# First cross attention: the last group of batches is projected in two tiles of four batches, the first tile's products placed ahead of the last two batches' probabilities

## The chip, the cores and the metric

The kernel runs on one core of a Trainium2 chip. The metric is the device time of one execution in microseconds; the figure that counts is the median of several executions.

## The reference: what is computed

Two layers over x (64 batches of 32 rows, 256 wide) with a context of 257 rows per batch. Each layer is a cross attention, a self attention and a feed-forward part, each added to x. The change lies in the first cross attention alone. Its latents are the layer-normed rows of x, its keys and values come from the normed context and from the latents themselves, with 16 heads of 64:

```python
xn = layernorm(x, ln_x_g, ln_x_b)            # context, 257 rows
ln = layernorm(latents, ln_l_g, ln_l_b)      # 32 rows
q = (ln @ Wq).reshape(b, m, h, d).transpose(0, 2, 1, 3)
kv = jnp.concatenate([xn @ Wkv, ln @ Wkv], axis=1)
kv = kv.reshape(b, n + m, 2, h, d)
k = kv[:, :, 0].transpose(0, 2, 1, 3)
v = kv[:, :, 1].transpose(0, 2, 1, 3)
qn = rmsnorm(q, qn_g) * scale
kn = rmsnorm(k, kn_g)
sim = jnp.einsum('bhid,bhjd->bhij', qn, kn)
...
attn = jax.nn.softmax(sim.astype(jnp.float32), axis=-1).astype(sim.dtype)
out = jnp.einsum('bhij,bhjd->bhid', attn, v)
out = out.transpose(0, 2, 1, 3).reshape(b, m, h * d)
return out @ Wout + bout
```

## The kernel before

The program is a row of stages; each has one stream of instructions per engine, written out by hand with semaphores, and ends in a barrier of all engines. The stage of the change is `cross_keyed`. The next is `self_attention`, whose first work on every engine stands behind that barrier.

`cross_keyed` goes through 64 batches (`n`) in 8 groups (`g`) of 8 (`GB`, place `j`). The values are never formed: the probabilities are multiplied with the normed context rows (`mix`), which gives 256 numbers per head and query, and the value and output weights are applied to a whole group at once (`project`). The order of the work on an engine is the order in which `group` calls the helpers. While batch n is finished, the batches behind it are prepared: keys of batch n+2 (`f.keys`, L382), transposed context rows of n+3 (L364), the spread of the key norms of n+1 (L409 transposes, L418 spreads them over the score columns through the two banks `key_bank`, ACT copies them out at L345), and raw rows of n+4. In the last group nothing of a next group is prepared (`is_in` is false past its end), so batch 62 has no keys to compute beside it, and batch 63 neither keys nor norms.

For one batch the chain is: `scores(n)` on PE (L1297, L1302) at the end of the batch before; maxima on DVE (L1112, L1115); exponentials on ACT (L1235); reciprocal and scaling on DVE (L1119, L1124) and the tail of the probabilities on POOL (L1200, L1202); transposes of the probabilities on PE (`probs_T`, L1313); high parts by ACT (L1242, L1244) and low parts by DVE (L1129, L1133); two times seven products on PE (`mix`, L1328), one half of the features each; both halves copied to the tile `mix` by ACT (L1249). POOL computes the key norms two batches ahead (L295, a power, then a split in three parts, L174 to L181).

After the eighth batch `project` (L1331 on) applies the value weights: four steps `i`, each with two pairs of heads, in the banks `key_bank[0]` and `key_bank[1]` in turn,

```python
mm = nc.tensor.matmul(key_bank[i % 2][half * DH:(half + 1) * DH, (pr % 2) * GT:(pr % 2 + 1) * GT],
                      wm.wv[:, f, h * DH:(h + 1) * DH], m.mix[:, f, place(h), :], start=(f == 0), stop=(f == FC - 1),
```

32 products of 256 tokens, with ACT copying the even steps to `oT` (L1278) and DVE the odd ones (L1164). Then the output weights: 2 tiles of 128 tokens, 8 products each (L1353), in the banks `out_bank` (banks 4 and 5 of the eight). Bank 4 is also the second bank of `mix`, bank 5 the one in which key norms are summed and transposed (`norm_bank`). DVE adds each tile to the residual (L1173). In all groups but the last the norm statistics for the next stage follow (`after.tile`); those of the last group are taken inside the next stage.

## Time and profile before

| | us |
|---|---|
| median of 3 runs | 2615.75 (2612.44 to 2619.3) |
| span of the profiled execution, first to last instruction | 2599.8 |
| time of the profiled execution | none is shown beside its span |
| PE busy | 2439.1 (94%) |
| DVE, POOL, ACT busy | 1696.2 (65%), 1474.8 (57%), 1282.3 (49%) |
| mean granted TensorE clock | 0.976 of full |

What stands in brackets behind a row is how long the engine was idle before it, and what ended that. The span does not hold the whole of a measured time: start and end of the program lie around it.

### The profile page before, as it was taken

How to read it: one execution, taken by the hardware profiler on the slowest of the kernel's cores; microseconds unless marked ns; L12 is line 12 of the kernel's file. 1: busy time of each engine (PE TensorE's matmuls, PEld its weight loads, DVE VectorE, ACT ScalarE, POOL GpSimd, SP SyncE). 2: the span in 40 equal slices, each digit the busy share in tenths (PEclk: the TensorE clock that was granted, in tenths of full speed). 3: DMA queues.
4: the chain of work that ended last, by engine and by line, in shares of the span. 5: the costliest groups of instructions: out<-in, count | busy, mean ns of one | idle time of the engine just before them, and what ended most of it. 6: DMA issues, size and time to landing. Idle time of an engine off the chain costs nothing. (4 is left out here: it accounts for less than half of the span.)

```text
span 2599.8 us, 64316 instructions
## 1 busy us (share of the span) xinstructions
PE 2439.1 (94%) x24498; PEld 1902.3 (73%) x24513; DVE 1696.2 (65%) x3969; ACT 1282.3 (49%) x2972; POOL 1474.8 (57%) x1669
## 2 busy tenths in 40 slices
PE   6998999999999999998797999699999999998997
PEld 3456888878787878886565588578888888886665
DVE  5777878686867777774575844476656655653665
ACT  3665656565656565654342333254445444543343
POOL 6996757676767576764662254675456544332233
PEclk9999999999999999998997999799999999999998
DMA  5332211111112121110003469533234323210001
GB/s 186 122 139 61 61 40 40 40 44 37 48 32 50 32 48 36 44 32 8 30 5 106 132 194 309 176 112 87 71 83 102 86 68 85 72 45 15 3 4 35
DMA packets 224819, 190.03 MB, mean 73 GB/s; under 512 B 89218, under 2 KB 212675, under 8 KB 224515
## 3 DMA queue, kind: packets, MB, share of 16 engines
q1 hardware_dynamic: 208994, 153.92, 19.9%
q0 software_dynamic: 9216, 27.28, 4.4%
q10 hardware_dynamic: 6304, 4.72, 0.6%
q8 instruction: 198, 3.24, 0.5%
q14 instruction: 107, 0.87, 0.1%
HBM read 151.53 MB, written 34.31 MB: 71 GB/s over the span
## 5 line engine op out<-in xcount | busy, mean ns | idle before, releaser
L295 POOL TENSOR_TENSOR rk<-ss,neg_half 128x32 f32<-128x32 f32 x64 | 348.8, 5449 | 246.5 <-DVE ss L277 246.5
L1784 PE MATMUL banks<-rowsT,qk 128*128 128x257 f32 x1024 | 243.1, 380 | 0.9 <-ACT qk L1704 0.9
L328 ACT ACTIVATE ksq<-kT 128x512 f32<-128x512 f32 x256 | 161.1, 629 | 162.5 <-DVE kT L271 162.5
L271 DVE COPY kT<-banks 128x512 f32<-128x512 f32 x256 | 176.6, 691 | 60.1 <-PE banks L382 56.0
L382 PE MATMUL banks<-x_hi,wk_hi 128*128 128x256 f32 x1024 | 213.2, 289 | 2.1 <-DVE kT L271 2.0
L1784 PEld LDWEIGHTS banks<-rowsT,qk 128*128 128x128 f32 x1024 | 189.2, 190 | 27.4 <-ACT qk L1704 1.2
L382 PE MATMUL banks<-x_hi,wk_lo 128*128 128x256 f32 x1024 | 206.7, 284 | 0.0
L382 PE MATMUL banks<-x_lo,wk_hi 128*128 128x256 f32 x1024 | 205.6, 282 | 0.5 <-DVE x_lo L263 0.5
L1235 ACT ACTIVATE score<-score,ntop 128x289 f32<-128x289 f32 x256 | 135.4, 530 | 115.5 <-DVE ntop L1115 115.3
L1593 POOL DMA_INDIRECT parts<-scratch_expert,address x128 | 131.5, 1028 | 91.0 <-DVE residual L1487 45.5
L1622 POOL CAST r_hi<-diff 128x512 fp32r<-128x512 f32 x64 | 43.3, 676 | 243.3 <-PE banks L1810 242.5
L382 PEld LDWEIGHTS banks<-x_hi,wk_hi 128*128 128x128 f32 x1024 | 159.2, 189 | 4.9 <-issue 4.4
L382 PEld LDWEIGHTS banks<-x_lo,wk_hi 128*128 128x128 f32 x1024 | 159.9, 190 | 0.8 <-DVE x_lo L263 0.7
L382 PEld LDWEIGHTS banks<-x_hi,wk_lo 128*128 128x128 f32 x1024 | 158.5, 188 | 0.0
L1685 ACT ACTIVATE prob<-banks,ntop 128x257 f32<-128x257 f32 x256 | 120.2, 479 | 72.9 <-DVE ntop L1505 72.9
L1505 DVE TENSOR_REDUCE ntop<-banks 128x2 f32<-128x514 f32 x128 | 88.4, 691 | 99.6 <-PE banks L1784 99.6
L1112 DVE CUSTOM_DVE_ANT_0 score<-banks,rkb 128x289 f32<-128x289 f32 x256 | 107.8, 457 | 63.4 <-PE banks L1302 55.1
L1693 ACT CAST p_hi<-banks 128x512 fp32r<-128x512 f32 x128 | 68.7, 589 | 161.8 <-PE banks L1793 154.9
L1249 ACT COPY mix<-banks 128x512 f32<-128x512 f32 x128 | 75.1, 587 | 112.6 <-PE banks L1328 112.6
L1810 PE MATMUL banks<-p_hi,r_hi 128*128 128x512 f32 x256 | 112.0, 438 | 3.5 <-ACT p_hi L1693 3.5
L1518 DVE TENSOR_TENSOR p_lo<-banks,p_hi 128x512 fp32r<-128x512 f32 x128 | 82.3, 685 | 49.8 <-ACT p_hi L1693 49.8
L1328 PE MATMUL banks<-p_hi,r_hi 128*128 128x512 f32 x256 | 114.5, 447 | 0.0
(362 smaller groups left out, 6546.4 us busy)
## 6 DMA issues: line engine op xcount, KB each, us to landing
rowsT<-in_ctxT SPq DMA_DIRECT2D x64, 257.0 KB, 2.9
wgu<-in_expert_gu SPq DMA_DIRECT2D x64, 256.0 KB, 4.0
rows<-in_ctx SPq DMA_DIRECT2D x64, 256.0 KB, 3.2
raw<-in_ctx SPq DMA_DIRECT2D x61, 256.0 KB, 2.7
scratch_qT<-qT SPq DMA_DIRECT2D x16, 512.0 KB, 2.6
scratch_kT<-kT SPq DMA_DIRECT2D x16, 512.0 KB, 3.0
q<-scratch_qT SPq DMA_DIRECT2D x64, 128.0 KB
kT<-scratch_kT SPq DMA_DIRECT2D x64, 128.0 KB
```

What stands on the lines that cost most here:

```text
L271: nc.vector.tensor_copy(m.kT[:, k, 2 * i:2 * i + 2, 0:ROWS], banks[i % 2].rearrange("p (a r) -> p a r", a=2)).then_inc(s.kT, 1)
L295: nc.gpsimd.tensor_tensor(m.rk[:], m.ss[:], kit.neg_half[:, 0:KF * H], ALU.pow).then_inc(s.rk, 1)
L328: nc.scalar.activation(m.ksq[:, 2 * i:2 * i + 2, :], m.kT[:, k, 2 * i:2 * i + 2, 0:ROWS], ACT.Square).then_inc(s.ksq, 1)
L382: mm = nc.tensor.matmul(banks[i % 2][:, a * ROWS:(a + 1) * ROWS], w[:, f, pr * P:(pr + 1) * P], x[:, k, f, :], start=(at == 0), stop=(at = ...
L1112: nc.vector.tensor_tensor_reduce(m.score[:, c, :], score[c][:, 0:NK], m.rkb[:, c, :], 1.0, -3.0e38, ALU.mult, ALU.max, m.top[:, c:c + 1]). ...
L1235: nc.scalar.activation(m.score[:, c, :], m.score[:, c, :], ACT.Exp, bias=m.ntop[:, c:c + 1], accum_out=m.mass[:, c:c + 1]).then_inc(s.p, 1)
L1328: mm = nc.tensor.matmul(mix_bank[f], lhsT, rhs, start=(at == 0), stop=(at == len(terms) - 1))
L1505: nc.vector.tensor_reduce(m.ntop[:, n % 2, h * HALF:(h + 1) * HALF], score[h][:, :, 0:CTX], AX.X, ALU.max, negate=True).then_inc(s.ntop, 1)
L1593: nc.gpsimd.indirect_dma_start(m.parts[:, t % 2, c, :], None, d.expert_rows, bass.IndirectOffsetOnAxis(kept.address[:, t, c:c + 1], 0)).th ...
L1685: nc.scalar.activation(m.prob[:, k, c, :], score[h][:, c - h * HALF, 0:CTX], ACT.Exp, bias=m.ntop[:, k, c:c + 1], accum_out=m.mass[:, k, c ...
L1784: mm = nc.tensor.matmul(score[h][:, c - h * HALF, 0:CTX], m.qk[:, f, j, c * BT:(c + 1) * BT, :].rearrange("p h q -> p (h q)"), m.rowsT[:, ...
L1810: mm = nc.tensor.matmul(kit.bank[3][:, f, :], lhsT, rhs, start=(at == 0), stop=(at == len(terms) - 1))
```

## The change

The last group no longer calls `project`. A tile is four batches, 128 tokens. Two new helpers stand in its place on PE. `tile_heads(t)` applies the value weights to tile t: bank 0 gets head pairs 0 to 3, bank 1 pairs 4 to 7, 32 products of 128 tokens. ACT copies the first bank, DVE the second. `tile_sum(t)` applies the output weights to tile t, 8 products, and DVE adds the tile. For tile 0, `tile_heads` is called at the head of batch 62 and `tile_sum` at the head of batch 63; both for tile 1 behind batch 63. Tile 0 goes to bank 5, tile 1 to bank 4. PE's spread of batch 63's norms, which writes the banks of the heads, waits for both copies.

```diff
@@ DVE
+                def tile_heads(i):
+                    dve.wait_ge(s.o_ps, LAST * (NP_ // 2) + (2 * i + 2))
+                    nc.vector.tensor_copy(m.oT[:, PER:NP_, i * P:(i + 1) * P], key_bank[1].rearrange("p (a t) -> p a t", a=PER)).then_inc(s.o_dve, 1)
+
+                def tile_sum(i):
+                    n = LAST * (GT // P) + i
+                    dve.wait_ge(s.x_ps, n + 1)
+                    nc.vector.tensor_tensor(X[:, n, :], X[:, n, :], out_bank[1 - i][:, 0:D], ALU.add).then_inc(s.x_add, 1)
...
+                        if n == B - 2:
+                            tile_heads(0)
                         probs_low(n)
+                        if n == B - 1:
+                            tile_sum(0)
...
+                    if g == LAST:
+                        tile_heads(1)
+                        tile_sum(1)
+                        return
@@ ACT
+                def tile_heads(i):
+                    act.wait_ge(s.o_ps, LAST * (NP_ // 2) + (2 * i + 1))
+                    nc.scalar.copy(m.oT[:, 0:PER, i * P:(i + 1) * P], key_bank[0].rearrange("p (a t) -> p a t", a=PER)).then_inc(s.o_act, 1)
...
                             exps(n, 1)
+                        if n == B - 2:
+                            tile_heads(0)
...
+                    if g == LAST:
+                        tile_heads(1)
+                        return
@@ PE
+                def tile_heads(t):
+                    done = LAST * GB + (t + 1) * (GB // 2)
+                    pe.wait_ge(s.mix0, done)
+                    pe.wait_ge(s.mix1, done)
+                    pe.wait_ge(s.rkb, (B - 1 + t) * 2)
+                    for i in range(2):
+                        for pr in range(PER * i, PER * (i + 1)):
+                            for half in range(2):
+                                h = 2 * pr + half
+                                for f in range(FC):
+                                    mm = nc.tensor.matmul(key_bank[i][half * DH:(half + 1) * DH, (pr % PER) * P:(pr % PER + 1) * P],
+                                                          wm.wv[:, f, h * DH:(h + 1) * DH], m.mix[:, f, place(h), t * P:(t + 1) * P], start=(f == 0), stop=(f == FC - 1),
+                                                          skip_group_check=True)
+                        mm.then_inc(s.o_ps, 1)
+
+                def tile_sum(t):
+                    pe.wait_ge(s.ss, B)
+                    pe.wait_ge(s.rkT, B)
+                    for pr in range(NP_):
+                        if pr % PER == 0:
+                            pe.wait_ge(s.o_dve if pr else s.o_act, LAST * (NP_ // 4) + (t + 1))
+                        mm = nc.tensor.matmul(out_bank[1 - t][:, 0:D], m.oT[:, pr, t * P:(t + 1) * P], wm.wo[:, pr, :], start=(pr == 0), stop=(pr == NP_ - 1))
+                    mm.then_inc(s.x_ps, 1)
...
                         n, k = g * GB + j, j % 2
+                        if n == B - 2:
+                            tile_heads(0)
+                        if n == B - 1:
+                            tile_sum(0)
...
+                            if n == B - 2:
+                                pe.wait_ge(s.o_act, LAST * (NP_ // 4) + 1)
+                                pe.wait_ge(s.o_dve, LAST * (NP_ // 4) + 1)
                             f.spread(n + 1)
...
-                    project(g, is_in(GB))
+                    if g == LAST:
+                        tile_heads(1)
+                        tile_sum(1)
+                        return
+                    project(g)
```

`LAST` is 7 and `PER` is 4. The other groups run as before. The same places in the built programs, line numbers being those of each file:

PE of the kernel before, from the scores of batch 62 (`kT,q`) over the norm transposes (`ident,rk_99`) and the transposes of batch 62's probabilities to the first mask product of batch 63; of the 14 mix products the first and the last are shown.

```order
L1302 MATMUL banks<-kT,q 32x289 x16
L409 MATMUL banks<-ident,rk_99 128x128 x2
L1313 MATMUL banks<-ident,prob 128x128 x12
L418 MATMUL banks<-rkT,sel 128x256 x4
L1328 MATMUL banks<-p_hi,r_hi 128x512
...
L1328 MATMUL banks<-p_tail,tails 128x512
L1297 MATMUL banks<-mask,one 128x289 x4
L1302 MATMUL banks<-kT,q 32x289 x16
L1313 MATMUL banks<-ident,prob 128x128 x12
```

PE of the changed kernel, the same place (here L1330 is the score product, L1341 the transposes of the probabilities, L1356 `mix`).

```order
L1330 MATMUL banks<-kT,q 32x289 x16
L1394 MATMUL banks<-mix,wv 64x128 x32
L409 MATMUL banks<-ident,rk_99 128x128 x2
L1341 MATMUL banks<-ident,prob 128x128 x12
L418 MATMUL banks<-rkT,sel 128x256 x4
L1356 MATMUL banks<-p_hi,r_hi 128x512
...
L1356 MATMUL banks<-p_tail,tails 128x512
L1325 MATMUL banks<-mask,one 128x289 x4
L1330 MATMUL banks<-kT,q 32x289 x16
L1405 MATMUL banks<-wo,oT 128x256 x8
L1341 MATMUL banks<-ident,prob 128x128 x12
```

Two blocks came in: 32 head products between the scores and the norm transposes of batch 62, and 8 output products between the scores and the probabilities of batch 63. Behind batch 63 PE has `L1345 MATMUL banks<-mix,wv 64x256 x32` and `L1353 MATMUL banks<-wo,oT 128x256 x16` in the kernel before, and 32 products of 64x128 and 8 of 128x256 now.

DVE of the changed kernel, from the scaling of batch 62's probabilities to its low parts.

```order
L1127 TENSOR_SCALAR prob<-score,rmass 128x256 x2
L1140 COPY oT<-banks 128x4x128
L1132 TENSOR_TENSOR p_lo<-banks,p_hi 128x512 x2
L1136 TENSOR_TENSOR p_tail<-banks,p_tail 33x512
L1115 ISA score,top<-banks,rkb 128x289
```

The copy of tile 0's second bank came in ahead of the low parts; the kernel before has none there.

## Rows read from the trace of the kernel before

**Rows 1.** The page, part 1, TensorE: busy us, share of the span, instructions.
```profile
PE 2439.1 (94%) x24498; PEld 1902.3 (73%) x24513; DVE 1696.2 (65%) x3969; ACT 1282.3 (49%) x2972; POOL 1474.8 (57%) x1669
```

**Rows 2.** Timeline, PE, batches 62, 63: start, us, engine, line, ..., [idle before <-releaser].
```profile
1198.57 0.39 PE L409 MATMUL banks<-ident,rk 128*128 128x128 bf16 x2 [4.38 <-POOL rk L181]
...
1206.32 0.30 PE L1297 MATMUL banks<-mask,one 1*128 1x289 bf16 x4
...
1212.19 2.82 PE L1313 MATMUL banks<-ident,prob 128*128 128x128 f32 x12 [4.43 <-DVE prob L1124]
...
1219.10 0.40 PE L1328 MATMUL banks<-p_tail,tails 128*128 128x512 f32 x1
```

**Rows 3.** Short windows, PE: length, busy (instructions), granted clock, DMA share, GB/s.
```profile
1197.00:1197.50 0.50, 0.00 (x0) 0.59 0.00 0
...
1203.50:1204.00 0.50, 0.50 (x3) 0.58 0.00 0
...
1210.50:1211.00 0.50, 0.00 (x0) 0.74 0.00 0
...
1236.00:1237.00 1.00, 0.00 (x0) 1.00 0.04 8
...
1238.00:1239.00 1.00, 0.85 (x3) 0.53 0.60 91
```

**Rows 4.** Timeline of the last projection: PE, then DVE.
```profile
1220.22 7.15 PE L1345 MATMUL banks<-mix,wv 128*64 128x256 f32 x64 [0.72 <-issue]
1227.30 7.17 PE L1353 MATMUL banks<-wo,oT 128*128 128x256 f32 x32
...
1234.51 0.42 DVE L1173 TENSOR_TENSOR residual<-residual,banks 128x256 f32<-128x256 f32 x1 [3.03 <-PE banks L1353]
```

**Rows 5.** Timeline, PE, batch 61, the last with keys to compute.
```profile
1186.19 0.28 PE L409 MATMUL banks<-ident,rk 128*128 128x128 bf16 x2
1186.32 1.48 PE L1313 MATMUL banks<-ident,prob 128*128 128x128 f32 x12
1187.73 0.39 PE L418 MATMUL banks<-rkT,sel 32*128 32x256 bf16 x4
1188.05 1.07 PE L394 MATMUL banks<-ksq,heads 128*32 128x256 f32 x16
1189.05 0.50 PE L1328 MATMUL banks<-p_hi,r_hi 128*128 128x512 f32 x1
...
1190.79 0.38 PE L402 MATMUL banks<-ident,sums 128*128 128x128 f32 x2
1190.93 0.48 PE L1328 MATMUL banks<-p_hi,r_hi 128*128 128x512 f32 x1
...
1192.42 0.40 PE L1328 MATMUL banks<-p_tail,tails 128*128 128x512 f32 x1
1192.75 0.30 PE L1297 MATMUL banks<-mask,one 1*128 1x289 bf16 x4
```

**Rows 6.** Lines L1345, L1353: duration ns min/median/max, first and last start, form.
```profile
L1345 PEld LDWEIGHTS banks<-mix,wv x512: 132/137/138, 330.5 to 1226.8; 128*64 128x64 f32 x171
...
L1353 PEld LDWEIGHTS banks<-wo,oT x256: 186/190/190, 337.6 to 1233.9; 128*128 128x128 f32 x128
L1353 PE MATMUL banks<-wo,oT x256: 379/379/483, 337.6 to 1234.1; 128*128 128x256 f32 x128
```

**Rows 7.** Timeline, batch 62: ACT, DVE, POOL.
```profile
1189.45 1.08 ACT L345 COPY rkb<-banks 128x512 f32<-128x512 f32 x2
...
1197.74 0.61 DVE L1124 TENSOR_SCALAR prob<-score,rmass 128x256 f32<-128x256 f32 x2
...
1199.68 0.21 POOL L1202 TENSOR_TENSOR prob<-score,rmass 128x12 f32<-128x12 f32 x1
```

**Rows 8.** Timeline, ACT, batch 63.
```profile
1213.40 0.59 ACT L1242 CAST p_hi<-banks 128x512 fp32r<-128x512 f32 x1 [2.39 <-PE banks L1313]
...
1219.53 0.59 ACT L1249 COPY mix<-banks 128x512 f32<-128x512 f32 x1 [1.05 <-PE banks L1328]
```

More of the change, by code:

```diff
@@ L1068, in uses @@
             return g * (GB // buffers) + (j // buffers + 1)
+        LAST = NG - 1
+        PER = NP_ // 2
         def groups(engine, group):
@@ L1173, in group @@
                         nc.vector.tensor_tensor(X[:, g * (GT // P) + i, :], X[:, g * (GT // P) + i, :], out_bank[i][:, 0:D], ALU.add).then_inc(s.x_add, 1)
-                    if g + 1 < NG:
-                        for i in range(GT // P):
-                            after.tile(dve, g * (GT // P) + i, s.x_add, g * (GT // P) + (i + 2))
+                    for i in range(GT // P):
+                        after.tile(dve, g * (GT // P) + i, s.x_add, g * (GT // P) + (i + 2))
                 dve.wait_ge(s.set, 5)
@@ L1329, in mix, with project @@
                     mm.then_inc(s.mix_ps, 1)
-                def project(g, more):
+                def project(g):
                     pe.wait_ge(s.mix0, (g + 1) * GB)
                     pe.wait_ge(s.mix1, (g + 1) * GB)
-                    pe.wait_ge(s.rkb, (g + 1) * (GB * 2) + (2 if more else 0))
-                    pe.wait_ge(s.ss, (g + 1) * GB + (2 if more else 0))
+                    pe.wait_ge(s.rkb, (g + 1) * (GB * 2) + 2)
+                    pe.wait_ge(s.ss, (g + 1) * GB + 2)
                     for i in range(NP_ // 2):
```

## The prediction

> **What bounds the kernel now.** The page first: TensorE (PE) is busy 94% of the span [rows 1], so time is saved where PE works longer than it must or stands idle with nothing else on the path. Next the timeline of the stretch that the change touches, batches 62 and 63 and the projection behind them [rows 2]; its brackets tell how long PE stood idle and for whom. Twice it was 4.4 us. Scores of batch 62 end 4.38 us ahead of 1198.57, at 1194.2, and PE goes on when POOL's split of the key norms of batch 63 is done; scores of batch 63 end 4.43 us ahead of 1212.19, at 1207.8, and the transposes of its probabilities wait for VectorE (DVE), which had to find the maxima, and for ScalarE's (ACT) exponentials between. The next stage begins behind a barrier, so what ends sooner here ends sooner altogether.
>
> **The change part by part.** The sum needs no recount of arithmetic: 64 passes of 256 columns become 128 of 128, 32 output passes stay 32. What counts is where they lie.
>
> *First tile's heads, ahead of batch 62.* 64 passes of 64 x 128. No row of before has this form in bulk, so it is bounded. Below: half of the 256-column pass, (1227.30-1220.22)/64 = 0.1106 us, so 0.055. Above: 0.1106, if halving the columns saves nothing because something else sets the pace. Nearest is the 128-column transpose with 128-column weights, 12 in 1.41 us (1186.32 to 1187.73) or 0.1175 [rows 5]; a 64-wide half fills half the array, and its load is shorter by 53 ns (190 to 137 ns, [rows 6]), so I take half of that: **0.059 us**. Tile: 64 x 0.059 = 3.8 us. PE is free at about 1194.1, so it ends near 1197.9, ahead of 1198.57: hidden in the hole with 0.7 us to spare. Its waits are met: mixes 56 to 59 were copied long before, and batch 62's spread norms, which held the two key banks, left by 1190.53 [rows 7]. On ACT the copy of the first bank (0.59) stands behind batch 62's exponentials, which DVE's scaling of 1197.74 waited for, and ahead of the cast of the norms that PE transposes only from 1198.57: free. On DVE the other copy (0.69) stands behind the scaling that ends at 1198.35 and ahead of the low parts, which wait for transposes and a cast: free. PE's new wait for both copies, ahead of the spread, ends near 1199.1; the spread stands behind all 12 transposes, which end after 1200 in any case [rows 7]. POOL and SP keep their order.
>
> *Batch 62 at full clock.* Term A. In batch 61, at full clock, the way from the first norm transpose to the mask product of the scores is 1186.19 to 1192.75 = 6.56 us, less key sums (1.00) and their transposes (0.14), which batch 62 lacks: 5.42 [rows 5]. Batch 62 took 1198.57 to 1206.32 = 7.75 [rows 2]. The last four transposes wait for POOL's tail, which ends at 1199.89 [rows 7], 0.25 later than a fast PE would ask: 7.75 - 5.42 - 0.25 = **2.1 us**.
>
> *First tile's sum, ahead of batch 63's probabilities.* 16 passes at (7.17-0.38)/31 = 0.219 us from start to start [rows 4, 6] = 3.5 us in a hole of 4.43: hidden, 0.9 to spare. Its two waits on the norm bank were met ahead of batch 62's spread. DVE's addition (0.42) lies between low parts and later work that waits for PE: free.
>
> *Batch 63 at full clock.* Term B. From the first transpose (1212.19) to ACT's copy of the second mix (1219.53) it took 7.34 us [rows 2, 8]. At full clock: first bank after 0.47 us (a third of 1.41), 0.35 to ACT (here 1.21 from the first transpose, less four of the twelve that took 2.82 at half clock with their drain), copy 0.59, then DVE's two low parts (1.29) and the tail part (0.69), with 0.1 for hand-overs: the tail product starts at 3.5; behind it itself (0.23), seven products whose last starts 1.49 on, as in batch 61, and 0.43 to the copy: 5.65. Saved: **1.7 us**. DVE, and no longer PE, is what is late here.
>
> *Second tile at the end.* Heads: 3.8 instead of 7.1 us, **3.3 us** saved (the first bank's copy lies under the second bank's products, the second's, 0.69, under the four first head pairs of the sum, 1.75). Sum: 16 passes instead of 32, **3.5 us** saved.
>
> Sum: 2.1 + 1.7 + 3.3 + 3.5 = **10.6 us**. The profile has a span of 2599.8 us; no time of its own is shown for that execution, and the runs' median, 2615.75, lies 16 us above the span. That surrounding part is not touched, so 2615.75 - 10.6 = **2605.1 us**, 0.41% less. Three runs of before spread by 3.4 us to either side; a change under 0.3%, 7.8 us, cannot be told from none.
>
> **A page against the trace.** The 53 ns by which a 64-column load is shorter than a 128-column one, and a 128-column pass of some 107 ns (half of a 256-column one's 0.214 to 0.219), would give 0.080 us per pass if a load could not lie under a product of the same half of the array. By the same arithmetic the 256-column passes would take (0.053+0.214)/2 = 0.134; they took 0.1106 [rows 4, 6]. So I leave loads hidden. The Trainium skill, page "TensorE: Matmul & The Clock Gate", says in "The mechanism" that a weight load overlaps matmuls in flight only when the row group differs, and in "Back-to-back issue gap" that a sustained stream of 128-column matmuls with loads runs at about 81 ns each. By that page a tile of heads would take 64 x 0.081 = 5.2 us and the gain be 8.7 us, an estimate from its figure. The trace speaks against the first rule, and does not show the second.
>
> **The rivals.** With p the price of one 128-column pass, a first tile that no longer fits its hole (p over 0.070) leaves a gain of 3.8 (A and B) + 7.1 - 64p + 3.5 - (64p - 4.5) + 0.25 (POOL's tail is then done before PE asks) = 19.1 - 128p us.
> 1. *Pace not halved.* Loads or issue set it, p between 0.080 and 0.1106. At 0.080 the gain is 8.9; at 0.1106 it is 4.9, 2610.9 us. For it: no row shows the form. Against it: 128-column weights with 128 columns already run at 0.1175 [rows 5], and a 64-wide load is the shorter one [rows 6]. Chance of a p near the upper end: 0.12.
> 2. *The clock falls all the same.* Remaining idle of 0.7 us and 0.9 us, with thin work around, could still let it drop; then A and B are gone: 6.8 us, 2608.9 us. Against it: behind the last output product PE was idle for 2.7 us, and the clock of 1236 to 1237 is still 1.00 [rows 3]. Chance 0.12.
> 3. *Slower.* Loads lie bare ahead of each pass: 0.137 + 0.107 = 0.244 us, the first tile takes 15.6 us in a hole of 4.5, everything of batch 62 on every engine stands behind it, and the gain turns into a loss of 12.1 us, 2627.9 us. It decides from p = 0.15 on (0.21 to be measured). Against it: the 0.1175 of [rows 5]. With it I count that the next stage, started elsewhere against its own clock falls (half clock from 1238.5 in before, [rows 3]), loses what was won. Chance 0.06.
> 4. *The change doesn't do what it says.* The built order has the products where the text puts them, so this is left with the 2% or so in case 3.
>
> **How the numbers follow.** Forecast 0.70; rivals 0.12, 0.12, 0.06. In the forecast the runs' spread (3.4 us) against a margin of 10.6 - 7.8 = 2.8 leaves some 0.17 of it inside 0.3%. Faster: 0.70 x 0.83, plus a third of rival 2 and a tenth of rival 1: 0.63. Slower: 0.06. Within: 0.31. The range goes from 2605.1 less the spread and 2 us for the next stage, 2599.5, to rival 1's 2610.9 and 1.1 us of spread, 2612.0; at either side about 0.1 is left out.
>
> **What would show it.** In the changed profile: 64 passes of 64 x 128 within 3.8 us from 1194.1, 16 output passes of 3.5 us behind the scores of batch 63, no row of the granted clock under 1.00 between 1194 and 1224, transposes of batch 63 from 1210.1, the last addition at 1223.8 and the next stage's first row 10.6 us sooner. A first tile of more than 4.5 us, a late first norm transpose, or a clock row at 0.50 behind it would show rival 1 or 2; an exponential or a cast on ACT waiting for the new copy would show a cost that I put at nothing.

## The result, and the profile after

| | before | changed |
|---|---|---|
| median of 14 runs, us | 2611.13 | 2599.97 |
| ratio of the times, 95% interval | | 0.9948 (0.9934 to 0.9961) |
| profiled execution: time, span | span 2599.8 | 2586.15, 2583.9 |
| PE busy, mean granted clock | 2439.1, 0.976 | 2436.0, 0.976 |

The change makes the kernel faster by 0.52% (0.39 to 0.66), some 13.6 us of 2611. The medians differ by 11.2; the ratio is near that of the means (2611.7 and 2597.9), which three runs of the changed kernel near 2587 pull down. The median of the 14 runs of before lies 4.6 us below that of the three known ahead.

From here on *the stretch* is the time from the first norm transposes of batch 61 to the first transposes of the next stage (L2373 in before, L2436 in the changed kernel). In before it is 1237.18 - 1186.19 = 50.99 us, in the changed kernel 1224.09 - 1183.70 = 40.39: 10.6 us less.

The page, part 1, of the changed kernel, beside [rows 1]:

```profile
PE 2436.0 (94%) x24562; PEld 1900.6 (74%) x24577; DVE 1692.7 (66%) x3969; ACT 1281.2 (50%) x2972; POOL 1469.5 (57%) x1669
```

PE has 64 more matmuls and 64 more weight loads, 128 instructions, and is busy for 3 us less: a first hint that part of the gain is clock.

The timeline of the changed kernel, PE, then ACT and DVE, from the first tile to the next stage (start, length, engine, line, operation, tiles, idle time before it and what ended it):

```profile
1191.62 3.77 PE L1394 MATMUL banks<-mix,wv 128*64 128x128 f32 x64
1196.08 0.28 PE L409 MATMUL banks<-ident,rk 128*128 128x128 bf16 x2 [0.69 <-POOL rk L181]
...
1201.83 0.30 PE L1325 MATMUL banks<-mask,one 1*128 1x289 bf16 x4
1203.20 3.72 PE L1405 MATMUL banks<-wo,oT 128*128 128x256 f32 x16
1207.70 1.53 PE L1341 MATMUL banks<-ident,prob 128*128 128x128 f32 x12 [0.79 <-DVE prob L1127]
...
1211.14 0.49 PE L1356 MATMUL banks<-p_tail,tails 128*128 128x512 f32 x1 [0.22 <-DVE p_tail L1136]
...
1213.99 3.74 PE L1394 MATMUL banks<-mix,wv 128*64 128x128 f32 x64 [0.72 <-issue]
1217.65 3.72 PE L1405 MATMUL banks<-wo,oT 128*128 128x256 f32 x16
1224.09 0.41 PE L2436 MATMUL banks<-ident,xl 128*128 128x128 f32 x2 [2.71 <-DVE xl L163]
...
1213.30 0.58 ACT L1268 COPY mix<-banks 128x512 f32<-128x512 f32 x1 [1.04 <-PE banks L1356]
...
1221.41 0.42 DVE L1145 TENSOR_TENSOR residual<-residual,banks 128x256 f32<-128x256 f32 x1 [2.96 <-PE banks L1405]
```

Against [rows 2] and [rows 4]: the first tile takes 3.77 us for 64 passes, 0.0585 each (1213.99 to 1217.65 for the second: 0.0572), and PE still waits 0.69 us for POOL where it waited 4.38; the sum leaves 0.79 of 4.43. The transposes of batch 63 take 1.53 us instead of 2.82.

Short windows of the changed kernel, PE: length, busy (matmuls), granted clock, DMA share, GB/s.

```profile
1196.00:1197.00 1.00, 0.92 (x10) 1.00 0.00 0
...
1209.00:1210.00 1.00, 1.00 (x7) 1.00 0.00 0
```

All 32 windows of 1 us from 1192 to 1224 read 1.00, where [rows 3] has the clock on its way to half speed (0.59 and 0.74 in windows in which it changed) behind both holes.

But 10.6 us is not 13.6. The profiled spans differ by 15.9 us, so the rest of the program is not the same either. The stage behind, the first self attention, from its first transposes to the start of its last output product, before and changed (length, then busy time of PE, PEld, DVE, ACT, POOL with instructions, clock, DMA share, GB/s):

```profile
1237.18:1406.60 169.42, 132.30 (x4447) 95.42 (x4448) 102.12 (x210) 63.13 (x144) 103.58 (x52) 0.91 0.05 14
```
```profile
1224.09:1381.30 157.21, 132.85 (x4448) 95.49 (x4448) 102.03 (x210) 62.98 (x144) 103.72 (x52) 0.91 0.05 15
```

Same instructions (the trace of before lacks one matmul's record), same busy times on all engines within 0.6 us, same clock, and 12.2 us less. The waits of PE in that stage, before and changed (engine, tile, line, releaser: us in total, times, longest):

```profile
PE banks L2452 <- issue: 15.2, 14, 2.4
PE banks L2438 <- issue: 7.1, 6, 2.5
```
```profile
PE banks L2515 <- issue: 5.9, 11, 2.1
PE banks L2501 <- issue: 5.2, 6, 1.8
```

L2515 is L2452 and L2501 is L2438 in the shifted file. "issue" is time in which PE waited for nothing that the profile shows. Over the stage it adds up to 25.4 us before and 12.8 now: the whole of the difference. Where those gaps lie, in before, PE:

```profile
1394.93 0.70 PE L2438 MATMUL banks<-kT,qT 32*32 32x32 f32 x42 [2.50 <-issue]
1395.56 2.08 PE L2462 MATMUL banks<-flat,yT 128*128 128x256 f32 x4
1397.57 1.06 PE L2452 MATMUL banks<-pT,v 32*32 32x32 f32 x81
1400.77 0.61 PE L2452 MATMUL banks<-pT,v 32*32 32x32 f32 x47 [2.14 <-issue]
```

From gap to gap there are 42 + 4 + 81 = 127 matmuls. Through the stage the gaps stand 126 to 128 matmuls apart, or two or three times as many; each matmul has a weight load, so that is about 256 instructions or a multiple. If gaps come at fixed positions of PE's instruction stream, 128 more instructions ahead move them to other products of the stage, dense ones or ones that a gap doesn't hurt. That was the theory for the second half of the experiments.

### The profile page after: what moved, and what is told of

It reads as the page before. It is cut to its first block and busy times, and to the rows that moved or that the text cites. A ratio compares the mean times of both kernels' runs of the same rounds, so it can differ in the third digit from the quotient of the medians.

```text
span 2583.9 us, 64446 instructions
## 1 busy us (share of the span) xinstructions
PE 2436.0 (94%) x24562; PEld 1900.6 (74%) x24577; DVE 1692.7 (66%) x3969; ACT 1281.2 (50%) x2972; POOL 1469.5 (57%) x1669
## 5 line engine op out<-in xcount | busy, mean ns | idle before, releaser
L328 ACT ACTIVATE ksq<-kT 128x512 f32<-128x512 f32 x256 | 161.1, 629 | 161.2 <-DVE kT L271 161.2
L1356 PE MATMUL banks<-p_hi,r_hi 128*128 128x512 f32 x256 | 113.4, 443 | 0.0
```

The costliest lines, as they stand in the source:

```text
L328: nc.scalar.activation(m.ksq[:, 2 * i:2 * i + 2, :], m.kT[:, k, 2 * i:2 * i + 2, 0:ROWS], ACT.Square).then_inc(s.ksq, 1)
L1356: mm = nc.tensor.matmul(mix_bank[f], lhsT, rhs, start=(at == 0), stop=(at == len(terms) - 1))
```

## The experiments

Each ratio is against the kernel before on the same chip. e1 to e4 ran on one chip (before: median 2597.14), r1 to r4 on a second (2597.87), s1 to s3 on a third (2613.44), s4 on a fourth (2614.64). *Attention* is the first self attention as bounded above, *issue* PE's idle time of that kind in it, *shift* the number of matmuls and weight loads added ahead of it.

| run | shift | stretch | attention | issue | ratio (95%) |
|---|---|---|---|---|---|
| before, profile | 0 | 50.99 | 169.4 | 25.4 | |
| changed, profile | 128 | 40.39 | 157.2 | 12.8 | 0.9948 (0.9934, 0.9961) |
| e1_both_tiles_at_end | 128 | 50.53 | 160.9 | 17.4 | 0.9986 (0.9972, 0.9999) |
| e2_sum0_at_end | 128 | 44.86 | 157.8 | 12.9 | 0.9956 (0.9940, 0.9972) |
| e3_before_filled | 160 | 47.26 | 161.1 | 17.0 | 0.9985 (0.9973, 0.9997) |
| e4_heads0_twice | 256 | 42.94 | 167.8 | 21.1 | 0.9953 (0.9937, 0.9968) |
| r1_before_again | 0 | 49.72 | 168.5 | 26.4 | 0.9996 (0.9982, 1.0011) |
| r2_after_again | 128 | 40.39 | 156.5 | 15.0 | 0.9951 (0.9933, 0.9970) |
| r3_before_padded | 128 | 51.21 | 161.1 | 15.3 | 0.9975 (0.9959, 0.9991) |
| r4_attention_filled | 128, then 160 | 40.38 | 159.7 | 17.1 | 0.9961 (0.9948, 0.9974) |
| s1_before_pad64 | 64 | 49.46 | 164.0 | 17.6 | 0.9977 (0.9962, 0.9992) |
| s2_before_pad192 | 192 | 49.56 | 160.6 | 17.7 | 0.9987 (0.9973, 1.0002) |
| s3_after_pad64 | 192 | 40.38 | 163.1 | 21.9 | 0.9941 (0.9919, 0.9963) |
| s4_before_pad256 | 256 | 51.36 | 172.0 | 24.4 | 0.9990 (0.9976, 1.0004) |

### The stretch: is it the place, and is it the clock?

**e1_both_tiles_at_end.** The changed kernel with both tiles behind batch 63, so that only the form of the products is changed and nothing moved.

```diff
 PE
-                        if n == B - 2:
-                            tile_heads(0)
-                        if n == B - 1:
-                            tile_sum(0)
...
                     if g == LAST:
+                        tile_heads(0)
+                        tile_sum(0)
                         tile_heads(1)
                         tile_sum(1)
```

The same on ACT and DVE; PE's wait for the two copies goes too.

> Both tiles are projected behind batch 63 (heads 0, sum 0, heads 1, sum 1); both holes are empty again. The stretch from the norm transposes of batch 61 to the next stage's first transpose was 50.99 us in before and 40.39 in the changed kernel. My theory (work hidden in the holes, and the clock held up by it): nothing is left of the gain, 51 to 52 us here, since 3.7+3.7+3.7+3.7 us of tiles take the place of 14.1 and both batches run at half clock again. Rival (the tiling itself shortens the tail): 46 us or less. Ratio to before 0.999 to 1.001 by my theory.

Measured: stretch 50.53. PE of e1, timeline:

```profile
1195.53 0.40 PE L409 MATMUL banks<-ident,rk 128*128 128x128 bf16 x2 [4.38 <-POOL rk L181]
...
1216.22 3.77 PE L1391 MATMUL banks<-mix,wv 128*64 128x128 f32 x64
1219.91 3.72 PE L1402 MATMUL banks<-wo,oT 128*128 128x256 f32 x16
1223.57 3.77 PE L1391 MATMUL banks<-mix,wv 128*64 128x128 f32 x64
1227.26 3.72 PE L1402 MATMUL banks<-wo,oT 128*128 128x256 f32 x16
```

The holes are back (4.38), and two tiles cost 14.7 us from 1216.22 to the end, against 14.25 in [rows 4]. Halving the width saves nothing: all of the stretch's gain comes from the place. The 50.53 lie a little under the 51 to 52 expected, inside the spread of before's stretch (49.5 to 51.4, see below). Yet the kernel as a whole is 0.14% faster than before (0.01 to 0.28); the attention is 8.5 us shorter with 128 more instructions ahead.

**e2_sum0_at_end.** Heads of tile 0 in the first hole, its sum at the end: the second hole stays open.

```diff
 PE, and DVE's addition alike
-                        if n == B - 1:
-                            tile_sum(0)
...
                     if g == LAST:
+                        tile_sum(0)
                         tile_heads(1)
```

> Heads of the first tile ahead of batch 62 as in the changed kernel, its sum behind batch 63 (there it can lie under the 0.7 us that the last mix copy takes). The hole ahead of batch 63 is empty again. By my terms: A (2.0) and the heads (3.4) stay, B (1.7) goes, the sum's 3.5 comes back less 0.7: the stretch is 50.99 - 2.0 - 3.4 - 0.7 = 44.9 us, with the clock at 1.00 through batch 62 and at 0.50 from the first transposes of batch 63. If the clock stayed up by some other cause, batch 63 would keep its 5.6 us (7.3 in before) and the stretch be 43.2.

Measured: stretch 44.86; in e2's timeline batch 63 is the old one:

```profile
1208.69 2.82 PE L1340 MATMUL banks<-ident,prob 128*128 128x128 f32 x12 [4.43 <-DVE prob L1127]
```

So the second hole is worth 44.86 - 40.39 = 4.5 us and the first 50.53 - 44.86 = 5.7. The terms have 5.4 (A with the heads, 2.1 + 3.3) for the first and 5.2 (B with the sum) for the second: each hole holds its product time and its clock loss. The 0.7 us missing at the second is what the expectation of e2 named: moved to the end, the sum runs where PE was idle for 0.72 us before the last heads.

**e3_before_filled.** The kernel before, with idle products of the same forms in both holes: 64 passes of 64x128 and 16 of 128x256, all on data that is ready, into banks that are free. Their results are not read, and the whole projection still stands at the end.

```diff
 PE of before
+                def filler_heads():
...
+                    for i in range(2):
+                        for pr in range(4 * i, 4 * i + 4):
+                            for half in range(2):
+                                h = 2 * pr + half
+                                for f in range(FC):
+                                    nc.tensor.matmul(key_bank[i][half * DH:(half + 1) * DH, (pr % 4) * P:(pr % 4 + 1) * P],
+                                                     wm.wv[:, f, h * DH:(h + 1) * DH], m.mix[:, f, place(h), 0:P], start=(f == 0), stop=(f == FC - 1),
...
+                def filler_sum():
...
+                    for pr in range(NP_):
+                        nc.tensor.matmul(out_bank[1][:, 0:D], m.oT[:, pr, 0:P], wm.wo[:, pr, :], start=(pr == 0), stop=(pr == NP_ - 1))
...
+                        if n == B - 2:
+                            filler_heads()
+                        if n == B - 1:
+                            filler_sum()
```

> The kernel before, with its projection untouched, and idle products put in both holes: 32 of 64x128 ahead of batch 62 and 8 of 128x256 ahead of batch 63, whose results nobody reads. It adds 7.4 us of TensorE work and takes nothing away. If the clock is what A and B are made of, the stretch falls by 3.7 us to 47.3, batch 62 takes 5.75 from norm transposes to scores (7.75 in before) and batch 63 5.6 (7.34). If A and B came from anything else in the change, the stretch stays at 51 or grows.

Measured: stretch 47.26. PE of e3, timeline, then the windows of the two stretches, before and e3 (columns as above):

```profile
1191.11 3.77 PE L1365 MATMUL banks<-mix,wv 128*64 128x128 f32 x64
1195.56 0.28 PE L409 MATMUL banks<-ident,rk 128*128 128x128 bf16 x2 [0.69 <-POOL rk L181]
...
1213.48 7.15 PE L1345 MATMUL banks<-mix,wv 128*64 128x256 f32 x64 [0.72 <-issue]
```
```profile
1186.19:1237.18 50.99, 38.75 (x278) 29.39 (x277) 17.21 (x49) 18.44 (x42) 14.01 (x22) 0.87 0.01 3
```
```profile
1183.19:1230.45 47.26, 41.91 (x359) 31.66 (x357) 17.02 (x49) 18.04 (x42) 14.01 (x22) 1.00 0.01 3
```

7.5 us of products whose results nobody uses are added, PE's busy time rises by only 3.2 because the rest runs at 2.4 GHz, and the stretch is 3.7 us *shorter*. That is A + B (3.8) by itself. Nothing is spared here but clock. Against the mean of six stretches with cold holes (50.4) it is 3.1: from the first norm transpose to the mask product batch 62 takes 6.8 to 8.0 us in them, in e3 and in the changed kernel 5.76 and 5.75.

**e4_heads0_twice.** The first tile's heads are computed twice in the first hole, 128 passes; the second time overwrites the first with the same values.

```diff
-                    for i in range(2):
+                    times = 0
+                    for i in (0, 1, 0, 1) if t == 0 else (0, 1):
...
-                        mm.then_inc(s.o_ps, 1)
+                        times += 1
+                        if t == 1 or times > 2:
+                            mm.then_inc(s.o_ps, 1)
```

> The changed kernel with the first tile's heads computed twice, 128 passes instead of 64 ahead of batch 62. The price per pass (0.0585 us in the changed kernel) and the hole (4.46 us from the tile's start to the norm transposes) give 7.5 us in 4.5: the norm transposes come 3.0 us late, 0.2 us comes back as POOL's tail is then done, and the stretch is 40.39 + 2.8 = 43.2 us. If the tile's passes cost other engines something too (ports, copies that come late), it is longer than 43.5.

Measured: stretch 42.94, 2.55 more than the changed kernel. PE of e4:

```profile
1192.32 7.26 PE L1395 MATMUL banks<-mix,wv 128*64 128x128 f32 x128
1199.52 0.28 PE L409 MATMUL banks<-ident,rk 128*128 128x128 bf16 x2
```

128 passes take 7.26 us, 0.057 each, and end past POOL's split, so no wait is left. Of 3.5 us more work 0.7 went into idle time and 0.2 into the wait for POOL's tail, 2.6 into the time. By the formula for a tile that no longer fits it would be 2.8; it holds to 0.3 us.

### The stage behind: is it the position of PE's instructions?

Two theories for the 12 us: *position* (gaps every 256 PE instructions, which any added instructions move) and *chance or start* (the stage differs from run to run, or with when and how its engines come in).

**r1_before_again and r2_after_again.** The two kernels unchanged but for an empty line.

```diff
     return res.results[0]["out_x"].reshape(B, S, D)
+
```

> The kernel before, unchanged. Its own trace and times beside the other runs of it: stretch 51.0 us, ratio 1.000 within its interval. What is asked is the self attention behind it, from its first transpose to its last output product: 169.4 us in the trace of before, 157 to 168 in the five others, and always 144 us plus PE's idle time on issue. If that time is scatter of one execution, this one lies anywhere in 155 to 170. If it belongs to the program, it is 169 again.

> The changed kernel, unchanged, on the same chip. Stretch 40.4 us. By my terms the ratio is 0.9959 (10.6 us); the first measurement said 0.9948 (0.9934 to 0.9961). If 3 us more come from the self attention behind it as a property of the program, the ratio is again 0.995 or less and its self attention takes 157 us again; if they were scatter, the ratio lies nearer to 0.996 and the self attention anywhere in 155 to 170.

Measured: attention 168.5 and 156.5 (169.4 and 157.2 the first time), ratios 0.9996 and 0.9951. It repeats in a second trace of each, so it is a property of each program, not chance. The stretch of the changed kernel repeats to 0.01 us, that of before doesn't (50.99, 49.72): in before the clock came back 5.4 us after PE resumed in one and 3.6 in the other (1203.9 behind 1198.57, 1200.9 behind 1197.24), so that term A is 2.0 us against the one and 1.1 against the other.

**r3_before_padded.** The kernel before with 64 tiny products in the first hole, 128 instructions with their loads; results not read.

```diff
+                        if n == B - 2:
+                            pe.wait_ge(s.rkb, (B - 1) * 2)
+                            for _ in range(64):
+                                nc.tensor.matmul(key_bank[0][0:S, 0:1], wk.sel[0:S, 0, 0:S], m.rkT[0:S, 0:1], start=True, stop=True)
```

> The kernel before with 64 tiny bf16 products (32 rows, one column) ahead of batch 62: 128 PE instructions more, just as many as the tiles add in the changed kernel, whose results nobody reads and which do next to no work. If the place of the instructions behind them (their supply) changes the self attention, its time moves clear of 169 and the ratio to 0.998 to 0.999; if not, the ratio is 1.000 less what the clock gives. The stretch tells the clock apart: 51.0 if such light work (about 1.6 us) does not hold it up ahead of batch 62, 49.0 if it does.

Measured: the stretch is as slow as before (51.21), the attention 161.1 instead of 169, issue 15.3 instead of 26. Nothing of the cross attention's work or order was touched, so the shift alone takes 8 us off the next stage and 0.25% off the kernel. Position holds; the start of the stage is as late and as cold as before. It gives 8 of the 12 us. Of the other 4 some 3 lie outside the issue time (161.1 - 15.3 = 145.8, against 142.9 in the mean of the changed kernel's two traces and 143.1 of before's), about what two traces of one kernel differ by (144.4 and 141.5), and stay open. The place matters down to a few instructions: r3 and e1, whose gaps lie four and two instructions behind those of the changed kernel (see below), have one of 2.6 us near matmul 411 of the stage, where the changed kernel and e2 have 0.2 to 0.5.

**s1_before_pad64, s2_before_pad192, s4_before_pad256.** The same edit with `range(32)`, `range(96)` and `range(128)`.

> The kernel before with 32 tiny bf16 products ahead of batch 62, 64 PE instructions more. In the traces so far the idle-on-issue gaps of the self attention stand 126 to 128 matmuls apart (256 PE instructions with their weight loads), and its time goes with the number of PE instructions put in ahead of it: 169 us at 0, 161 at 128, 161 at 160, 168 at 256. If the supply of PE instructions comes in pieces of 256 and what counts is where a piece ends within a step of the attention, 64 lies between 0 and 128, 163 to 167 us. If the 161 at 128 was chance, it is 168 to 170. Stretch 51 us either way.

> The same with 96 tiny products, 192 PE instructions more: by the theory of pieces between 128 and 256, 162 to 167 us for the self attention; by chance 168 to 170. The tiny products take 2.6 of the hole's 4.4 us; stretch 51 us if the clock still falls, 49 if they hold it up.

> The kernel before with 128 tiny bf16 products ahead of batch 62, 256 PE instructions more, that is one whole piece. By the theory of pieces everything behind stands as in the kernel before: the self attention takes 168 to 170 us again (169.4 and 168.5 at 0; 164.0, 161.1 and 160.6 at 64, 128 and 192), with 24 to 27 us of idle on issue, and the ratio is 0.999 to 1.001. If more instructions were simply better, or the shifts by 64 to 192 did something else, it stays at 160 to 164. The products take 3.5 of the hole's 4.4 us, so the clock may hold: stretch 49 to 51.

Measured, attention by shift in the kernel before: 0: 169.4 and 168.5; 64: 164.0; 128: 161.1; 192: 160.6; 256: 172.0. At 256 it is back where it started, and issue too (24.4). Two values miss what was expected, 192 by 1.4 us below its 162 to 167 and 256 by 2 above its 168 to 170. The windows of r3 and of s4, the attention of each:

```profile
1237.69:1398.80 161.11, 133.19 (x4448) 96.06 (x4448) 102.12 (x210) 63.09 (x144) 104.04 (x52) 0.92 0.05 15
```
```profile
1234.17:1406.20 172.03, 135.91 (x4448) 97.21 (x4448) 101.98 (x210) 63.13 (x144) 102.83 (x52) 0.87 0.05 14
```

s4 also ran at a lower clock there (0.87 against 0.92), so not all of its 172 is position. e4, the changed kernel with 256 in all, fell back as well: 167.8. One period of 256 instructions fits all of it.

**Where the gaps stand, and what ends them.** The kept traces settle more than the stage's time does. Count all that a trace lists of PE from the start of the attention: weight loads, matmuls and its sequencer's own instructions. Every gap on issue of 0.15 us or more then stands, to within one instruction, at one place past a multiple of 256: at 201 in before and r1, 137 in s1, 73 in r3, 9 in s2, 201 again in s4. In the changed kernel it is 69, which is 132 earlier and not 128, since the tiles bring four more instructions of the sequencer. There are 249 such gaps in the 14 traces and no exception. What comes in pieces of that size is on the page of the kernel before, among the DMA queues (packets, MB, share of 16 engines):

```profile
q8 instruction: 198, 3.24, 0.5%
```

Each packet has 16384 bytes, and 198 of them match the 50755 instructions that the trace has of PE (198.3 times 256); in every other trace the two agree to within one packet as well. This queue brings PE's instructions, 256 in a packet. The windows around the gap of 2.50 us ahead of 1394.93, in before (length, busy, clock, DMA share, GB/s); the 16 GB/s are one packet:

```profile
1392.00:1393.00 1.00, 0.43 (x42) 0.50 0.08 16
1393.00:1394.00 1.00, 0.00 (x0) 0.50 0.00 0
1394.00:1395.00 1.00, 0.07 (x9) 0.50 0.00 0
```

It was under way from 1392.33 to 1393.66, and PE went on 1.27 us later. Behind all 249 gaps PE went on 1.2 to 1.7 us after the last such packet had landed. So the gaps are PE waiting for its own instructions, and an edit ahead moves the products at which it has to wait.

**s3_after_pad64.** The changed kernel with 2 times 16 tiny products, shift 192 in all.

```diff
                         if n == B - 2:
+                            pe.wait_ge(s.rkb, (B - 1) * 2)
+                            for _ in range(16):
+                                nc.tensor.matmul(key_bank[0][0:S, 0:1], wk.sel[0:S, 0, 0:S], m.rkT[0:S, 0:1], start=True, stop=True)
                             tile_heads(0)
                         if n == B - 1:
+                            pe.wait_ge(s.ss, B)
+                            pe.wait_ge(s.rkT, B)
+                            for _ in range(16):
+                                nc.tensor.matmul(norm_bank[0:S, 511:512], wk.sel[0:S, 0, 0:S], m.rkT[0:S, 0:1], start=True, stop=True)
                             tile_sum(0)
```

> The changed kernel with 16 tiny bf16 products in front of each of the two early blocks, 64 PE instructions more (192 over the kernel before). They take 0.4 us of each hole, which has 0.7 and 0.8 to spare: stretch 40.4 us. By the theory of pieces the self attention leaves its 157 us, to 160 or more, unless the best place lies beyond 128, then it is below 157 and this version beats the changed kernel. By chance it stays at 157.

Measured: stretch 40.38, attention 163.1, 6 us above the changed kernel's, issue 21.9. The ratio, 0.9941 (0.9919 to 0.9963), is not worse than 0.9948: what the attention lost is not found in the whole. So a stage can't be tuned by padding and the sum be taken as gained; every stage behind is shifted too. No version here is distinguishable from the changed kernel for the better.

**r4_attention_filled.** The changed kernel with eight idle 128x256 products (32 instructions) in the 4.95 us hole at the head of the self attention. Is e3's effect to be had there too?

```diff
                 def step(n, has):
+                    if n == -2 and not rotary:
+                        for _ in range(8):
+                            nc.tensor.matmul(kit.psum(4)[:, 0:D], w[:, 0, 0:P], w[:, 0, 0:D], start=True, stop=True)
```

> The changed kernel with 8 idle products of 128x256 (16 passes, 3.5 us at full clock) in the next stage, in the hole of 4.95 us ahead of its first query and key transposes (PE waits there for POOL's 5.4 us power). In the changed kernel the clock was at half from there for some 6 us of nearly full PE work. By the clock theory these 6 us shrink to 3: the self attention is 3 us shorter than with the same idle time on issue, 141 plus issue instead of 144, and the transposes (8) take 1.1 instead of 2.0 us. Rival: the chain over POOL and DVE sets the pace there and nothing is won.

Measured: the transposes behind the hole in the changed kernel, then in r4:

```profile
1237.88 1.97 PE L2477 MATMUL banks<-ident,qk 128*128 128x128 f32 x8 [4.95 <-DVE qk L2226]
...
1245.66 1.06 PE L2477 MATMUL banks<-ident,qk 128*128 128x128 f32 x8
```
```profile
1237.27 1.09 PE L2477 MATMUL banks<-ident,qk 128*128 128x128 f32 x8 [1.50 <-DVE qk L2226]
...
1244.61 1.88 PE L2477 MATMUL banks<-ident,qk 128*128 128x128 f32 x8 [1.44 <-DVE qk L2226]
```

The first eight run at full clock, the next ones 7 us later are cold again. Over the whole stage nothing is won: less its issue time it takes 142.6 us, where the changed kernel has 144.4 and 141.5. But the 3 us were there for a while. Counted from the start of the stage, r4's second transposes come at 19.5 us (21.6 and 21.3 in the changed kernel's two traces) and its ninth at 77.8 (81.3 and 80.8). They went again behind a wait for instructions, at which the clock fell (timeline, then windows of r4):

```profile
1334.00 0.65 PE L2515 MATMUL banks<-pT,v 32*32 32x32 f32 x37 [2.22 <-issue]
```
```profile
1333.00:1334.00 1.00, 0.00 (x0) 0.75 0.00 0
1334.00:1335.00 1.00, 1.00 (x38) 0.50 0.00 0
```

It stayed down for 6.8 us; at this place the changed kernel's traces have none at half speed. Over the stage r4 spends 24.0 us at half speed, the changed kernel 27.3 and 21.9. So the fill bought what was expected of it, and r4 does not show how to keep it: with waits for instructions behind it, the clock falls at another place.

### Where the whole difference lies

Two traces of before (profile, r1) against two of the changed kernel (profile, r2), means in us: up to batch 61 1185.5 to 1184.5 (-1.0); stretch 50.4 to 40.4 (-10.0); first self attention 169.0 to 156.9 (-12.1); the rest of the span 1190.5 to 1199.8 (+9.3). Total -13.8, which agrees with 0.9948. Of the 9.3, the second self attention holds 3.7 (150.3 to 154.0, first to last output product). The other 5 or so build up between some 1510 and 1730 us, at the end of the first layer and the head of the second; over the 600 us behind that the distance changes by no more than 0.5 us. They are 7.0 us in the pair of the profiles and 2.9 in r1 and r2, and two traces of one kernel differ there as much: by 3.2 (before) and 7.4 (changed). r3, with nearly the changed kernel's position and on the chip of r1 and r2, has 1188.6 us behind the attention, r1 1187.6 and r2 1196.9. So neither that the 9.3 belong to the change nor that they come from the position is shown.

The times say how much is the stretch: e1, with a shift like the changed kernel's and a stretch like before's, is 0.14% or 3.6 us faster than before, the changed kernel 13.6, and the 10 between them are the stretch, within intervals of some 3.5 us to either side of each.

## Why the prediction was right or wrong

The stated range, 2599.5 to 2612.0, holds the median 2599.97 only by 0.5 us: the forecast, 2605.1, was 5.1 us too high, 4.6 of it in the base. Taken by the ratio, 2611.13 x 0.9948 = 2597.6 us, the result lies 1.9 us below the range. The predicted 10.6 us lie at the edge of what was measured (0.39 to 0.66% of 2611 is 10.2 to 17.2 us). The four terms came out; the step from their sum to the kernel's time didn't.

*First tile hidden, 0.059 a pass, 3.8 us, 0.7 to spare:* 0.0585, 3.77, 0.69. Right. The copies on ACT and DVE cost nothing, as said: the norm transposes follow POOL's split at once, and the spread stands behind the transposes. Rivals 1 and 3 fall with the pass price. The chosen row, half of a transpose with 128-column weights (0.1175), was a good neighbour: at 256 columns too a 64-wide pass takes half of a 128-wide one (0.1106 against 0.219).

*Term A, 2.1:* 7.75 became 1201.83 - 1196.08 = 5.75, so 2.0. *Term B, 1.7:* 7.34 became 1213.30 - 1207.70 = 5.60, so 1.74, and what is late inside is DVE's tail part, 0.22 us (L1136), as said. Rival 2 falls: no window under 1.00. e3 shows the two terms alone, 3.7.

*Heads 3.3:* 7.08 [rows 4] became 1217.65 - 1213.99 = 3.66, so 3.4. *Sum 3.5:* 7.21 became 1221.41 - 1217.65 = 3.76, so 3.45. The last addition starts at 1221.41; the 1223.8 named ahead had not allowed for a cross attention that began its last batches 2.5 us sooner (1183.70 against 1186.19), which is the variation of the 1184 us ahead of it.

*Slips in the text ahead:* by its own row the clock first falls at 1197.1, not 1197.4, which is 2.9 us after PE went idle; the next stage in before is at half clock from 1238.05, not 1238.5; the lower bound adds up to 2599.7, not 2599.5, and the last addition to 1223.9, not 1223.8. None changes a term.

*The failed step:* "That surrounding part is not touched, so 2615.75 - 10.6 = 2605.1". It is wrong in three ways.
- The base. The median of three runs lay 4.6 us above that of fourteen. And the 16 us between span and median were not start and end of the program: the changed kernel's profiled time, 2586.15, is 2.25 us above its span. The rest was spread of runs and chips, which I knew only as 3.4 us to either side: on the four chips of the experiments the median of before goes from 2597.1 to 2614.6.
- The rest of the program is not untouched when instructions are added to an engine. The self attention behind, with the same instructions and busy times, became 12 us shorter (r1, r2), 8 of it from the shift alone (r3), since PE waits there for its own instructions at places a multiple of 256 apart (249 gaps, each ending behind a packet of them); in the stages after it 9 us were lost, which is not shown to be the change's. The 2 us that I allowed for the next stage, and its clock as the reason, were the wrong size and the wrong cause: PE's "issue" time there was on view ahead of the prediction and I did not read that stage.
- The base scatters by itself. The stretch of before took 49.5 to 51.4 us in the six traces in which its holes held nothing or tiny products, and where I looked (before, r1) with the moment at which the clock came back. Against their mean, 50.4, the stretch gives 10.0, not 10.6.

*Rival 3* (apart from its pass price) counted in that the next stage loses what was won here. That stage did move, by as much as was won, but to the other side, and not by its clock (0.91 in both). *Rival 4* falls: both blocks stand where the order had them.

*The page against the trace:* the 81 ns of the Trainium skill's "TensorE: Matmul & The Clock Gate", "Back-to-back issue gap", would have made the tile 5.2 us, an estimate from its figure; it took 3.77, and 128 of the same passes 7.26. The rule of the Trainium skill's same page, "The mechanism", that a load overlaps products in flight only when the row group differs, doesn't hold for these products either: loads of 0.137 us on all rows lie beside passes that start every 0.0585 us. The same section names a background weight buffer as a second way, which would allow it; no run here tells whether that is what happened.

## What to carry to other kernels

Look for the places where PE waits for other engines with nothing of its own prepared, and fill them with work that has to be done anyway: here 7.5 us of products vanished in two holes of 4.4 us, and keeping the clock up gave another 3 to 4. Before adding the gain to a kernel's total, read the stages behind for PE idle time put down to "issue": instructions added to PE move it, by up to 12 us in one stage here, with either sign (s3 and e4 lost 6 and 11 us against the changed kernel), and the test is the same shift without the change (r3, e1), the sequencer's instructions counted in. Whether a fill pays is read at the end of the stage, not behind the hole (r4). Take the base from as many runs as the result will have.

## What the hardware showed that I had not expected

**PE waits for its own instructions, in pieces of 256.** In a stage of dense 32x32 products PE stands idle for up to 2.7 us at every 256th instruction or at multiples of that, 12.8 to 26.4 us in all. All 249 gaps of the 14 traces stand at such places, and each ends 1.2 to 1.7 us after a 16384-byte packet of the instruction queue has landed. The time of the stage returns after a shift of 256 instructions and is 8 us lower at half of it. Not shown is why the packet comes late at some of these places and in time at others.

**Busy with tiny products, and the clock still falls.** s4 fills 3.35 us of the first hole without a break; PE of s4, timeline and windows:

```profile
1190.72 3.35 PE L1362 MATMUL banks<-rkT,sel 32*32 32x1 bf16 x128
1195.17 0.40 PE L409 MATMUL banks<-ident,rk 128*128 128x128 bf16 x2 [1.10 <-POOL rk L181]
1195.36 2.77 PE L1313 MATMUL banks<-ident,prob 128*128 128x128 f32 x12
```
```profile
1192.00:1193.00 1.00, 1.00 (x46) 1.00 0.08 16
1194.00:1195.00 1.00, 0.07 (x3) 0.63 0.00 0
1195.00:1196.00 1.00, 0.83 (x6) 0.50 0.00 0
```

e3 has 64-wide products of 128 columns in the same hole, and the clock stays:

```profile
1192.00:1193.00 1.00, 1.00 (x23) 1.00 0.02 5
...
1195.00:1196.00 1.00, 0.44 (x5) 1.00 0.00 0
```

In both PE reads as fully busy at 1192 to 1193; s4's 12 transposes take 2.77 us, at 1.2 GHz, and those of the changed kernel 1.7. The last 1.10 us ahead of s4's transposes are idle against 0.69, but r4's longer 1.50 us behind eight wide products (16 passes of 256 columns) left the clock up. So two runs that fill the same hole, as busy by the profile but with different products, differ in the clock; why is not shown.
